# A state-space layer and a mixture of experts in one loop: the state sum is turned back one turn later, and the projections take other turns

## What is computed

```
x_ssm, x_gate = split(xn @ W_in + b_in)
x_conv = silu(conv(x_ssm));  B, C = split(x_conv @ W_bc + b_bc)
dt = softplus(x_conv @ W_dt + b_dt);  A = -exp(A_log)
h[t] = h[t-1] * exp(dt[t] * A) + dt[t] * x_conv[t] * B[t]      # 256 x 16 states
y[t] = sum over the 16 states of h[t] * C[t]  +  x_conv[t] * D
mamba = layernorm((y * silu(x_gate)) @ W_out + b_out + xn)

per token the 2 best of 8 experts, with weights:
ffn = layernorm(sum of w * (gelu(layernorm(xn @ w1 + b1)) @ w2 + b2) + xn)
out = x + mamba + ffn
```

## Time and profile before

| | |
|---|---|
| median of three runs | 1950.87 us |
| profiled execution | 1948.48 us, span 1946.7 us |
| PE busy | 1606.0 us, 82% |
| DVE busy | 1552.5 us, 80% |
| ACT busy | 1460.7 us, 75% |
| POOL busy | 972.6 us, 50% |
| mean granted clock of TensorE | 0.91 |

### The profile page before, as it was taken

One profiled execution on the slowest core, in us unless ns is written; L12 is line 12 of the kernel. 1 busy time (PEld: TensorE's weight loads), 2 busy tenths in 40 slices (PEclk: granted clock), 3 DMA queues, 4 the chain that ended last, 5 costly groups with the idle time before them and its releaser, 6 DMA issues. The chain is left out here.

```text
span 1946.7 us, 30665 instructions
## 1 busy us (share of the span) xinstructions
PE 1606.0 (82%) x6978; PEld 1002.4 (51%) x6979; DVE 1552.5 (80%) x2529; ACT 1460.7 (75%) x2553; POOL 972.6 (50%) x563
## 2 busy tenths in 40 slices
PE   5665637997989899979989898999899888976799
PEld 4443414555556556555555555565556555553344
DVE  4544437999899889989988998999899889941797
ACT  3333326988889798979888897989798878965576
POOL 2546464656556555556565565655565645632000
PEclk9767667999999899989999998999899999989799
DMA  7975473333333333333333333333333333322884
GB/s 239 292 259 194 171 243 95 96 105 92 84 82 105 77 90 90 95 86 92 105 90 83 86 103 79 91 88 95 85 94 102 83 84 91 105 55 37 281 269 151
DMA packets 183045, 235.72 MB, mean 121 GB/s; under 512 B 45882, under 2 KB 148541, under 8 KB 182864
## 3 DMA queue, kind: packets, MB, share of 16 engines
q1 hardware_dynamic: 141378, 172.36, 28.7%
q0 software_dynamic: 26160, 36.06, 10.2%
q10 hardware_dynamic: 15328, 25.20, 3.6%
HBM read 149.86 MB, written 83.70 MB: 120 GB/s over the span
## 5 line engine op out<-in xcount | busy, mean ns | idle before, releaser
L540 POOL TENSOR_TENSOR area<-area,more 128x1024 f32<-128x1024 f32 x258 | 603.7, 2357 | 600.6 <-DVE area L1275 317.1
L1296 DVE TENSOR_TENSOR area<-area,psD 128x1024 f32<-128x1024 f32 x256 | 311.4, 1217 | 75.6 <-PE psD L985 75.3
L962 PE MATMUL psH<-w_sb,ffn_xT 128*128 x544 | 276.1, 632 | 3.2 <-ACT ffn_xT L671 3.0
L972 PE MATMUL psX<-w_sb,h_T 128*128 x1088 | 275.1, 398 | 0.8 <-ACT y_out L677 0.8
L517 POOL DMA_INDIRECT expert_d<-y_out,meta x139 | 225.0, 1619 | 78.3 <-ACT y_out L677 52.1
L993 PE MATMUL psY<-ident,area 128*128 128x128 f32 x2048 | 250.7, 276 | 0.0
L695 ACT ACTIVATE h_T<-psT,be_T,g_T 128x128 f32<-128x128 f32 x540 | 202.3, 459 | 54.4 <-PE psT L952 53.7
L972 PEld LDWEIGHTS psX<-w_sb,h_T 128*128 128x128 f32 x1088 | 217.3, 202 | 31.8 <-issue 0.9
L993 PEld LDWEIGHTS psY<-ident,area 128*128 128x128 f32 x2048 | 222.2, 141 | 15.1 <-issue 3.6
L655 ACT ACTIVATE psD<-area,A_sb 128x512 f32<-128x512 f32 x258 | 177.7, 689 | 45.4 <-DVE area L1296 19.4
L509 POOL DMA_INDIRECT sorted_x<-area,place x128 | 127.7, 998 | 142.4 <-DVE place L1244 105.6
(11 more groups left out here) (188 smaller groups left out, 2560.1 us busy)
## 6 DMA issues: line engine op xcount, KB each, us to landing
more<-B_rows_d SPq DMA_DIRECT2D x130, 512.0 KB, 4.0
xin<-sorted_x SPq DMA_DIRECT2D x137, 128.0 KB
more<-ssm_d SPq DMA_DIRECT2D x18, 512.0 KB
area<-xnT_d SPq DMA_DIRECT2D x18, 512.0 KB
mamba_d<-mo_stage SPq DMA_DIRECT2D x17, 512.0 KB, 2.9
area<-L_attn_x SPq DMA_DIRECT2D x8, 1024.0 KB
xnT_d<-w_sb ACTq DMA_DIRECT2D x16, 512.0 KB, 3.5
expert_d<-area ACTq DMA_DIRECT2D x8, 1024.0 KB
```

The lines of the kernel that those rows point to most:

```text
L540: pool.tensor_tensor(inflow[:, k], dtx, B_rep[par][:, k].rearrange("p (a t) -> p a t", a=1).to_broadcast([P, KD, CHUNK]), ALU.mult).then_i ...
L962: nc.tensor.matmul(psH[:, :], ffn_xT[:, k, :], w1_sb[:, bass.ds(e, 1), k, :].rearrange("p o h -> p (o h)"), start=(k == 0), stop=False)
L972: nc.tensor.matmul(psX[:, DIM:2 * DIM], h_T[:, buf, k, :], w2_sb[:, bass.ds(e, 1), k, :].rearrange("p o d -> p (o d)"), start=(k == 0), st ...
L1296: V.tensor_tensor(h, h, C_rep[k].rearrange("p (a t) -> p a t", a=1) .to_broadcast([P, KD, CHUNK]), ALU.mult).then_inc(S[f"hC{k}_done"], 1)
```

## The change

The list of tasks starts with an empty turn: output 0 is projected in turn 1 and output 1 in turn 5 (before 0 and 1), the gate in turns 6 and 7 (before 5 and 6). Gate 1 is taken by ACT in turn 0 of the next chunk, and the silu of the gate follows at the end of turn 2 of that chunk. PE's turn 0 has `transpose_sum` in the task's place, and `add_up` stands at the end of every turn. DVE's `gate` stands in turn 1 between the two scans. ACT copies the sum after the tile's copy. SP stores the output in turn 7 (before 3) and loads xT in turn 0 (before: turn 7 of the chunk ahead). In front of the loop gate 1 comes last. Behind it the sum is turned back before the expert turns, and the last output is projected inside the first of them.

```diff
@@ -50,10 +50,10 @@
 PARTS = 3
 BC = 2 * STATE
 
-TASKS = ["out0", "out1", "bc", "dt0", "dt1", "gate0", "gate1", None]
+TASKS = [None, "out0", "bc", "dt0", "dt1", "out1", "gate0", "gate1"]
 BC_TAKEN = TASKS.index("bc") + 1
 CONV_TURN = 1
-GATE_TURN = 6
+GATE_TURN = 2
 DT_TAKEN = TASKS.index("dt1") + 1
 END_BUFS = 4
 END_RING = 8
@@ -393,7 +393,6 @@
 
             sp.wait_ge(S["gate_ready"], 2)
             sp.wait_ge(S["zero_fill"], 16 * 6)
-            load_chunk(1)
             load_ssm(1)
             store_B(0)
             load_B(0, 0, 0)
@@ -415,15 +414,15 @@
                             store_mamba(c)
                         if pr == CONV_TURN + 1:
                             load_ssm(c + 2)
-                        if pr == TASKS.index("gate1") + 1:
-                            sp.wait_ge(S["gate_ready"], 2 * c + 4)
-                            load_chunk(c + 2)
+                        if pr == 0:
+                            sp.wait_ge(S["gate_ready"], 2 * c + 2)
+                            load_chunk(c + 1)
             store_mamba(CHUNKS)
             for u in range(MAMBA_TURNS, FFN_TURNS):
                 load_tile(u + 2, (u + 2) % RING)
             sp.wait_ge(S["xin_loaded"], 32 * LOADED)
             sp.wait_ge(S["y_stored"], 16 * (FFN_TURNS + LAG + 2))
-            sp.wait_ge(S["xT_loaded"], 16 * (CHUNKS + 2))
+            sp.wait_ge(S["xT_loaded"], 16 * (CHUNKS + 1))
             sp.wait_ge(S["xpad_loaded"], 16 * (CHUNKS + 2))
             sp.wait_ge(S["mo_stored"], 16 * (CHUNKS + 1) + 16)
             sp.wait_ge(S["exp0_done"], KD * (MAMBA_TURNS + 1))
@@ -560,7 +559,7 @@
 
             pool.wait_ge(S["y_stored"], 16 * (FFN_TURNS + LAG + 2))
             pool.wait_ge(S["mo_stored"], 16 * (CHUNKS + 1) + 16)
-            pool.wait_ge(S["xT_loaded"], 16 * (CHUNKS + 2))
+            pool.wait_ge(S["xT_loaded"], 16 * (CHUNKS + 1))
             pool.wait_ge(S["exp0_done"], KD * (MAMBA_TURNS + 1))
             pool.wait_ge(S["exp1_done"], MAMBA_TURNS + 1)
             pool.wait_ge(S["dbx_done"], CHUNKS * STATE + 2 + 2)
@@ -760,8 +759,7 @@
 
             act.wait_ge(S["scattered_first"], 16 * 2 * FIRST)
             act.wait_ge(S["xn_stored"], 16 * FIRST_TURNS)
-            for name in ("gate0", "gate1"):
-                take(name, 0, 0)
+            take("gate0", 0, 0)
             conv_silu(0)
             with_exp()
             take("bc", 0, 0)
@@ -789,13 +787,17 @@
                         decay1_of(u + 1, state[1], par)
                         hidden_root(u)
                         if pr == 0:
-                            copy_sum(c)
-                        elif pr <= 2:
-                            take_out(c, pr - 1, psT[:, :])
+                            take("gate1", c, half)
+                        elif pr == TASKS.index("out0") + 1:
+                            take_out(c, 0, psT[:, :])
+                        elif pr == TASKS.index("out1") + 1:
+                            take_out(c, 1, psT[:, :])
                         elif TASKS[pr - 1] is not None:
                             take(TASKS[pr - 1], g, ahead)
                         decay0_of(u + 1, 1, state[0], g, par)
                         copy_xT(u + 1)
+                        if pr == 0:
+                            copy_sum(c)
                         if pr == BC_TAKEN + 1:
                             bc_middle(g, ahead)
                         if pr == DT_TAKEN:
@@ -810,6 +812,7 @@
                         if pr == GATE_TURN:
                             gate_silu_of(c, half)
                         with_exp()
+            take("gate1", CHUNKS, 0)
             copy_sum(CHUNKS)
             for u in range(MAMBA_TURNS, FFN_TURNS):
                 e, e_y = expert(u), expert(u - LAG)
@@ -1053,14 +1056,13 @@
 
 
             pe.wait_ge(S["ssm_taken"], 2 * KD * TURNS)
-            order = ["gate0", "gate1", "bc", "dt0", "dt1"]
+            order = ["gate0", "bc", "dt0", "dt1", "gate1"]
             for at, name in enumerate(order):
                 if at:
                     wait_taken(order[at - 1], 0)
                 task(name, 0)
                 if name == "bc":
                     ranks(TURNS - 1)
-            wait_taken("dt1", 0)
             pe.wait_ge(S["tables_ready"], 1)
             seed(None)
             spread_C0(0, 0, 0, 0)
@@ -1073,7 +1075,6 @@
             up(0, expert(0))
             transpose_x(1)
             pe.wait_ge(S["gate_zero"], 2)
-            transpose_sum(0)
             spread_C1(0, 1, 0)
             with pe.Fori(0, BATCH) as b:
                 for half in range(2):
@@ -1084,34 +1085,38 @@
                         state = [(pr * 2 + 2 + k) % STATE for k in range(2)]
                         par = half if pr < PAIRS - 1 else ahead
                         e_down, e_up = expert(u - 1), expert(u + 1)
-                        if pr > 0 and TASKS[pr - 1] is not None:
+                        if pr == 0:
+                            wait_taken("gate1", c)
+                        elif TASKS[pr - 1] is not None:
                             wait_taken(TASKS[pr - 1], g)
                         transpose_h(u)
                         up(u + 1, e_up)
-                        if pr == PAIRS - 1:
-                            add_up(u, pr % 2)
                         spread_C0(u + 1, state[0], par, g)
-                        if TASKS[pr] is not None:
+                        if pr == 0:
+                            transpose_sum(c)
+                        else:
                             pe.wait_ge(S["gelu_done"], u + 1 + 1)
-                        if pr < 2:
-                            project_out(c, pr, psT[:, :])
+                        if pr == TASKS.index("out0"):
+                            project_out(c, 0, psT[:, :])
+                        elif pr == TASKS.index("out1"):
+                            project_out(c, 1, psT[:, :])
                         elif TASKS[pr] is not None:
                             task(TASKS[pr], g)
                         transpose_x(u + 2)
                         spread_C1(u + 1, state[1], par)
-                        if pr == PAIRS - 1:
-                            transpose_sum(c + 1)
                         down(u - 1, (pr + 1) % 2, e_down)
                         if pr == 0:
                             seed(c)
-                        if pr != PAIRS - 1:
-                            add_up(u, pr % 2)
-            for j in range(2):
-                project_out(CHUNKS, j, psY[:, j * CHUNK:(j + 1) * CHUNK])
+                        add_up(u, pr % 2)
+            wait_taken("gate1", CHUNKS)
+            transpose_sum(CHUNKS)
             for u in range(MAMBA_TURNS, FFN_TURNS):
                 e_down, e_up = expert(u - 1), expert(u + 1)
                 transpose_h(u)
                 up(u + 1, e_up)
+                if u == MAMBA_TURNS:
+                    for j in range(2):
+                        project_out(CHUNKS, j, psY[:, j * CHUNK:(j + 1) * CHUNK])
                 transpose_x(u + 2)
                 down(u - 1, (u - 1) % 2, e_down)
             down(FFN_TURNS - 1, (FFN_TURNS - 1) % 2, expert(FFN_TURNS - 1))
@@ -1408,6 +1413,8 @@
                             u = c * PAIRS + pr
                             g, ahead = c + 1, 1 - half
                             scan0_of(u, pr * 2, half)
+                            if pr == 1:
+                                gate(c, ahead)
                             scan1_of(u, pr * 2 + 1, half)
                             if half == 0:
                                 keep_last(u, pr * 2)
@@ -1416,9 +1423,7 @@
                             hidden_norm(u)
                             times_C(u, pr * 2, 0, half)
                             if pr == CONV_TURN - 1:
-                                convolve(g, 0, range(0, 2))
-                                gate(c, ahead)
-                                convolve(g, 0, range(2, TAPS))
+                                convolve(g, 0)
                             if pr == CONV_TURN:
                                 convolve(g, 1)
                                 pad_left(half == 0)
```

## The result

The changed kernel takes 1981.16 us, the median of four runs (1967.16 to 1986.75), beside 1950.28 us (1946.87 to 1952.25) of the kernel before: a ratio of 1.0122, 95% interval 1.0080 to 1.0164. It is slower. The profiled execution is the shortest of the four, 1967.16 us with a span of 1965.4 us, so the trace explains 18.7 us against the profiled one of before (1948.48), not 31.

A forecast was written before the change was run, and what follows sets the result against it. It took DVE to lead, with ACT and PE close behind and a few us of slack a turn. 30.4 + 10.4 - 9 - 5 + 6 - 1.5 = +31.3 us gave 1982.2 us, range 1958 to 1994.

The forecast's parts named there:

- Silu in turn 2: ACT's turns 2 and 3: DVE's norm in turn 3 waits 1.9 us a chunk, never given back, +30.4 us.
- Output projection in turn 5: PE's turn 5: output projection takes 0.65 us longer than the gate's, DVE waits as much in 16 chunks, +10.4 us.
- worse: Rival: ACT's lag lasts into turn 4, or PE's gaps lower the clock; 1 us more a chunk, 1998 us, chance 0.11.
- Sum turned back in turn 0: Even turns 0 to 2: waits of 7.1 us go, a new one of 6.0 comes, -9 us in eight batches.
- S: Start of an even chunk's first scan on DVE; the branch was forecast to begin at S+5.6.
- w: DVE's new wait in even turn 1, at the gate, for the sum turned back; forecast 6.0 us.
- The odd chunks: PE's wait for the copied sum goes here too: 1.3 us in four of eight batches, -5 us.
- the start: In front of the loop: one load of xT is gone from in front of B's store, -1.5 us.
- the tail: Behind the loop: the sum comes after gate 1, so the last copy, store and tile load come later, +6 us.
- high clock: Rival: PE keeps 2.4 GHz after the branch, new wait 3.0 us, gain 33 instead of 9, 1958 us, chance 0.12.
- branch ready: Rival: the branch is ready when PE is, no new wait, gain 57 us, total 1934 us, chance 0.08.
- a first matmul before S+12.3 and the high clock: Condition, after the branch, for the change to be faster than before: the new wait under 2.1 us.

The follow-up runs named there:

- silu6: The changed kernel with the silu of the gate back at the end of turn 6: 1883.8 us, ratio 0.9944 to the kernel before.
- before_silu2: The kernel before with only its silu of the gate moved from turn 6 to turn 2: 1915.22 us, ratio 1.0111 to the kernel before.
- again: The changed kernel unedited, measured on another chip: 1903.24 us, ratio 1.0041 to the kernel before.
- fill: The changed kernel, with PE repeating turn 5's first spread six times in front of its wait for gelu: 1877.86 us, ratio 0.9928 to the kernel before.
- swap: The changed kernel with the gate's projection in PE's turn 5 again and output 1 in turn 6: 1879.54 us, ratio 0.9922 to the kernel before.
- pad: The changed kernel with twelve more PE transposes once in front of the loop, so the body's code lies further on: 1980.93 us, ratio 1.0133.
- unroll2: The changed kernel with PE's loop run four times over four halves, its branch only before batches 2, 4 and 6: 1951.68 us, ratio 0.9991 to before.
- both: The changed kernel with silu back in turn 6, gate projection in turn 5 and output 1 in turn 6: 1859.77 us, ratio 0.9833 to before.
- before_fill: The kernel before, with PE repeating the first spread of turns 4 and 5 six more times each: 1936.18 us, ratio 0.9900 to the kernel before.
- later_fill: both_later with PE repeating the first spread of turns 4 and 5 six more times each: 1889.1 us, ratio 0.9670 to the kernel before.
- both_later: The kernel both, with DVE's gate behind the second scan and the statistics of turn 1: 1846.47 us, ratio 0.9757 to the kernel before.
- again_b: The changed kernel unedited, measured once more on a third chip: ratio 1.0070 to the kernel before.

## Why the prediction was right, and where it was not

The total, 1982 for 1981.16, is closer than its terms deserve. In the profiled execution the change costs 18.7 us, in the medians 31, 10 and 14 in three measurements (ratios 1.0122, 1.0041, 1.0070). What makes the loss differ is open. The loop of the changed kernel is nearly the same in its three profiles (1427.7, 1429.3 and 1427.5 us from the first turn's start to the last's), but I have no profile of the kernel before on the other chips.

*Silu in turn 2: right mechanism, too large.* The norm of turn 3 waits 1.7 to 1.8 us, as forecast. The step that failed is "the loss is not repeated, but nothing returns it": turns 3 to 5 together are 1.1 us (even) and 0.6 us (odd) longer, 13.7 us in 16 chunks and not 30.4. DVE's norm and, in front of it, ACT's timeline in the changed kernel show the wait and why it can be given back:

```profile
972.67 0.81 DVE L1314 TENSOR_SCALAR h_norm<-psH,hmv,hrs 128x512 f32<-128x512 f32 x1 [1.83 <-ACT hrs L688]
```
```profile
967.90 1.06 ACT L748 ACTIVATE area<-area 128x1024 f32<-128x1024 f32 x1
968.97 1.28 ACT L699 ACT_TABLE_LOAD   x1
...
972.43 0.20 ACT L688 ACTIVATE hrs<-hln 128x1 f32<-128x1 f32 x1
```

ACT works through turns 3 and 4 without a pause, so DVE's later waits for PE, which is behind ACT's gelu, shrink: the second spread's in turn 5 falls from 1.1 (even) and 1.4 us (odd) to 0.5 and 0.6. That ACT's queue sets these turns is read from the rows; no run took ACT's work away there. By medians silu6 and before_silu2 put the move at 19 to 22 us. The difference to 13.7 lies in turn 6, where a low clock is more frequent with the silu's move (10 chunks in before_silu2 for 4 in the kernel before, 11 in again for 5 in silu6).

*Output projection in turn 5: right mechanism, too small.* 0.7 us a chunk is there (13.25 for 12.55), 10.4 forecast and 11 measured. But turn 6 is 23.3 us longer in all. The other 12 us are the low clock behind PE's wait of 1.9 us, which the forecast had only as the rival "worse". fill shows that the wait has its part in it, since turn 6 takes 13.2 us in all chunks once it is filled. These 12 us can't be booked to the projection alone, as the forecast's split would: the wait was there before (1.97 us, 4 chunks with a low clock in turn 6), the silu's move without the projection has 10 such chunks in before_silu2 and 5 in swap, the projection without the silu's move 5 in silu6, and both together 10 or 11.

*Sum turned back in turn 0: the sum was taken too dear.* The branch came at S+5.60 (1023.57), as forecast to the hundredth. The step that failed is "the first matmul follows 7.6 us later": it was 6.1 in the batch shown, w 4.08 for 6.0, and the even turns 0 to 2 gained 39.63 - 37.43 = 2.20 us a batch, 17.6 for 9. Why 7.6 became 6.1 is open: pad has 8.3 to 11.9 with the same loop body, so the number doesn't belong to the body alone, but no run moved the code of the kernel before alone. The odd chunks gave 4.5 for 5, the start 2.5 for 1.5, the tail 6.3 for 6.

With the loop's terms as measured, 13.7 + 23.3 - 17.6 - 4.5 = 14.9, as read. Against the profiled execution's 18.7 us the sum of 31.3 is 12.6 too high: 16.7 too much for turns 3 to 5, 8.6 too little gain for the sum's move, 12.9 too little for turn 6, and 0.2 in the rest. That the four runs' median nonetheless lies at 1981 is luck and no merit of the terms. The rival "high clock" is refuted by L965's 3.62 us and the window's 0.50; "branch ready" by the 4.08 us, though unroll2 shows that its mechanism is true once the branch is gone (31.3 - 48 is -16.7 there, not -16.5, which changes nothing). Its point "a first matmul before S+12.3 and the high clock" was met in the first half only. The forecast's chance of 0.11 for "worse" was too low for its mechanism, if not for its total.

The sum's move, with the start and the tail that go with it, is a gain of 1.7% (both). The kernel became slower by the silu and the projection that moved with it.

## What to carry to other kernels

Price a reordering by each move alone: one change had a gain of 32 us and two losses of 43 together in it. Where PE waits, look at the granted clock behind the wait, in every chunk and not in one: here the wait did not grow (1.97 us before, 1.89 after), but the low clock came more often. Cheap work that fills the wait can be worth more than it costs: in fill, before_fill and later_fill no chunk has a low clock in turns 5 and 6, and even the kernel before gains 1.0%. A number read off a loop's branch may hold only for the kernel in which it was read: keep some us of cover behind it, as both_later does, instead of counting on the last one measured.

## What the hardware showed that I had not expected

- The same branch at the same place in the program costs 5.3 to 11.9 us until the next matmul, from kernel to kernel. The Trainium skill (Runtime: NRT & Kernel Launch, Instruction fetch mechanics) says that instructions come in blocks of 16 KiB and that a taken branch outside two of them waits for its target; unroll2 agrees that the taken branch is what waits, and pad speaks for its place, though no run shows a block. The 108 ns that the Trainium skill gives for a compare-and-branch (Advanced Engine Details and Errata, Control Flow Timing) are near the loop's exit alone, 0.08 us; by their records the taken branches took 3.3 to 5.8 us.
- After a wait of 1.9 us PE's clock is low in some chunks and not in others. Chunks with a low clock in turn 6, one profile each: with the gate's projection 2 of 16 (both, both_later), 4 (before), 5 (swap) and 10 (before_silu2), with the output's 5 (silu6), 8 (pad), 10 (after, again_b), 11 (again) and 13 (unroll2). So the kind of projection doesn't settle it; what does is open.
- DVE's `bc_residue` takes 0.68 us in the median after the change, for 1.34 before, when it falls behind POOL's product and no longer beside it:

```profile
1066.22 0.68 DVE L1342 TENSOR_TENSOR more<-more 96x512 f32<-96x512 f32 x1
```

In the kernel both_later, where the silu is back in turn 6, the same line takes 1.34 us again. In all 14 profiles it takes 0.67 to 0.68 us where no product of POOL runs at the same time (142 times), 1.32 to 1.34 where one does for 0.77 to 0.79 us of it, and 1.60 to 1.63 where one does for 1.06 to 1.08 (48 times each). In both cases 0.54 to 0.55 us of it are left without POOL's product: it hardly gets on beside it. No run moved POOL's product by itself.
